# A transformer block on one core: a step order of its own for each engine, from a table of shifts

## What is computed

```python
x = x + layernorm(attention(layernorm(x)))      # 16 heads of 16 channels, rotary, causal softmax
x = x + layernorm(ffn(layernorm(x)))
# ffn(h): router (sigmoid, 4 groups of 4 experts, best 2 groups, best 4 experts of 16)
#         y = sum over the 4 picked experts of gate * (silu(h Wg) * (h Wu)) Wd
#         returns h + y + shared(h), shared(h) = (silu(h Ws_g) * (h Ws_u)) Ws_d
```

## Time and profile before

| what | value |
|---|---|
| median of 3 runs | 983.47 us (982.06 to 987.12) |
| span of the profiled execution | 1048.8 us |
| PE busy | 852.6 us, 81% |
| PEld busy | 615.2 us, 59% |
| DVE busy | 652.3 us, 62% |
| ACT busy | 456.3 us, 44% |
| POOL busy | 426.7 us, 41% |
| mean granted TensorE clock | 0.888 |

### The profile page before, as it was taken

The page is one execution under the profiler, slowest core; times in us unless marked ns, Lnnn a source line. Parts: engine busy times, 40 slices in busy tenths (PEclk is TensorE's granted clock), DMA queues, the critical chain, the costliest instruction groups (busy, mean ns, idle before and its releaser), DMA issues.

```text
span 1048.8 us, 20609 instructions
## 1 busy us (share of the span) xinstructions
PE 852.6 (81%) x6580; PEld 615.2 (59%) x6580; DVE 652.3 (62%) x1914; ACT 456.3 (44%) x763; POOL 426.7 (41%) x408
## 2 busy tenths in 40 slices
PE   4569798987987987987987877978977799989955
PEld 3436374664664663664654545757865588867722
DVE  5577658687687687687586674533642233687916
ACT  2115454544544544544543555425433355544410
POOL 3222113135335335335213234374565555664621
PEclk9759898997897897997987998889999999998978
DMA  4685726236336336336395212453545566997783
GB/s 161 147 222 144 216 64 163 75 98 174 98 99 173 99 99 173 98 81 172 98 322 159 85 47 92 144 167 93 166 150 161 161 178 164 383 314 281 247 339 128
DMA packets 89175, 168.72 MB, mean 161 GB/s; under 512 B 14704, under 2 KB 56688, under 8 KB 88816
## 3 DMA queue, kind: packets, MB, share of 16 engines
q1 hardware_dynamic: 75248, 128.85, 42.1%
q0 software_dynamic: 13824, 38.55, 9.9%
HBM read 90.15 MB, written 76.68 MB: 159 GB/s over the span
## 4 chain that ended last, share of the span: by engine, by line
PE 40%; DVE 23%; issue 11%; SPq 8%; DMA 6%; another core or an unknown queue 5%; ACT 4%; POOL 3%; DVEq 0%; ACTq 0%; POOLq 0%
DVE nmax L829 8%; PE ring L1536 6%; PE ring L1314 5%; PE ring L1316 4%; PE ring L1315 4%; PE ring L1392 3%; PE ring L1557 3%; PE ring L1358 2%; SPq L628 2%; PE ring L1383 2%; SPq L629 2%; DMA xg<-sorted_rows 2%; PE ring L1436 2%; PE ring L1522 2%
## 5 line engine op out<-in xcount | busy, mean ns | idle before, releaser
L1244 ACT ACTIVATE prob<-ring 128x1024 f32<-128x1024 f32 (+1 forms) x192 | 167.5, 881 | 215.5 <-PE ring L1383 196.5
L829 DVE TENSOR_REDUCE nmax<-ring 128x2 f32<-128x1024 f32 (+3 forms) x256 | 201.8, 819 | 73.3 <-PE ring L1365 43.6
L736 POOL DMA_INDIRECT expert_rows<-ys,dest x160 | 159.2, 995 | 127.0 <-ACT ys L1198 74.8
L728 POOL DMA_INDIRECT sorted_rows<-xr,idx_all x128 | 130.5, 1019 | 104.8 <-DVE xr L991 71.5
L1536 PE MATMUL ring<-we,xh 128*128 x640 | 160.3, 396 | 0.0
L1536 PEld LDWEIGHTS ring<-we,xh 128*128 128x128 f32 x640 | 121.6, 200 | 14.6
L1054 DVE SCALAR_TENSOR_TENSOR sl<-sl,got,ring 128x128 f32<-128x128 f32 x160 | 48.3, 343 | 109.8 <-ACT sl L1296 62.5
L1358 PE MATMUL ring<-k_st,q_st 48*128 48x512 f32 (+3 forms) x512 | 88.9, 387 | 26.0 <-issue 9.7
L1392 PE MATMUL ring<-prob,v_sb 128*32 128x512 f32 (+3 forms) x1024 | 106.3, 518 | 3.2 <-ACT prob L1244 3.2
L1377 PE MATMUL ring<-maskt_b,halves_b 64*128 64x128 bf16 (+2 forms) x768 | 58.4, 233 | 50.7 <-DVE nmax L829 23.5
L1377 PEld LDWEIGHTS ring<-maskt_b,halves_b 64*128 64x128 bf16 x768 | 22.8, 97 | 125.4 <-issue 56.7
(11 more groups left out here) (203 smaller groups left out, 1650.8 us busy)
## 6 DMA issues: line engine op xcount, KB each, us to landing
xg<-sorted_rows SPq DMA_DIRECT2D x160, 134.0 KB
parts<-part SPq DMA_DIRECT2D x32, 512.0 KB
ykt<-expert_rows SPq DMA_DIRECT2D x14, 1024.0 KB
k_st<-parts SPq DMA_DIRECT2D x64, 128.0 KB
q_st<-parts SPq DMA_DIRECT2D x64, 128.0 KB
we<-w_exp SPq DMA_DIRECT2D x1, 6144.0 KB
sorted_rows<-zeros SPq DMA_DIRECT2D x2, 2144.0 KB, 9.6
sorted_rows<-zeros SPq DMA_DIRECT2D x32, 134.0 KB
```

The lines of the kernel that those rows point to most:

```text
L728: pool.indirect_dma_start(out=xs[group_of(s)], out_offset=bass.IndirectOffsetOnAxis(ap=idx_all[:, s, t, k:k + 1], axis=0), in_=xr[:, s % 2 ...
L736: pool.indirect_dma_start(out=yk, out_offset=bass.IndirectOffsetOnAxis(ap=dest[:, j % 8, b:b + 1], axis=0), in_=ys[:, j % NYS, b, :], in_o ...
L829: dve.tensor_reduce(nmax[:, Q % 2, :, pp, qb], slot[:, :, col:col + (qb + 1) * P], AX.X, ALU.max, negate=True).then_inc(s_max, 1)
L1244: act_e.activation(prob[:, u % 2, 2 * half:2 * half + 2, 0:width], slot[:, :, 0:width], ACT.Exp, scale=SCALE).then_inc(s_exp, 1)
```

## The change

A table `MOVES` gives shifts in the units of the list. A key is (kind and part, engine or None for all, quad of the sequence 0 to 3 or None, sequence or None); the shifts of all keys that match are added. `make_plan` is now called once per engine, so each engine sorts its own list. Which quad or sequence a step belongs to comes from its number; the kinds in `FIXED_KINDS` (expert blocks, final sums, `DUM`, `PAD`, `WE`, `GE`, `GR`) don't move. No instruction is added, taken away or changed in size. The ring's rotation and PE's waits for it follow PE's list, the number that a DVE maximum waits for follows PE's list, and so on: each wait is counted in the order of the engine that raises it.

```diff
-def make_plan():
+MOVES = {
+    (('AT',), 'tensor', None, None): 0.01, (('AT',), 'vector', None, None): 0.1, (('AV', 0), 'tensor', 3, None): 0.5,
+    (('AV', 0), 'tensor', None, None): 0.1, (('AV', 0), None, None, None): 0.03, (('AV', 1), 'tensor', 1, None): 0.6,
...
+    (('GA', 0), 'scalar', None, None): -0.7, (('GA', 0), 'gpsimd', None, 7): -1.8, (('GA', 0), None, None, None): 0.5,
...
+    (('LG',), 'scalar', None, None): 0.2, (('LN',), 'gpsimd', None, None): 1.5, (('LNA',), 'vector', None, 7): -0.9,
+    (('LNA',), 'vector', None, None): -1.3, (('LNA',), 'gpsimd', None, None): -2.2, (('LNA',), None, None, None): 0.2,
+    (('LNB',), 'vector', None, 7): -0.7, (('LNB',), 'vector', None, None): -0.2, (('LNB',), None, None, None): -0.1,
+    (('LNC',), 'sync', None, None): -2.0, (('LNC',), None, None, None): 0.6, (('LNR',), 'scalar', None, None): 2.3,
...
+    (('LX',), 'sync', None, None): -2.7, (('MT',), 'vector', 3, None): -0.2, (('MT',), 'sync', None, None): 0.3,
+    (('MT',), None, 1, None): 0.11, (('MT',), None, None, 0): -0.16, (('MT',), None, None, 7): -0.2,
+    (('MT',), None, None, None): -0.1, (('OP',), None, None, None): -0.2, (('OT',), 'vector', 0, None): 0.2,
+    (('OT',), 'vector', 1, None): 0.3, (('OT',), 'vector', None, None): 0.2, (('OT',), None, 0, None): -1.5,
...
+    (('S', 1, 1), None, None, None): 0.15, (('S', 1, 2), None, 1, None): 0.2,
...
+    (('SC', 3, 3), None, None, None): 2.8, (('SPL', 0), 'gpsimd', None, None): -1.4, (('SPL', 0), None, None, 7): 0.5,
...
+    (('STL',), 'sync', None, 7): 0.9, (('STL',), 'sync', None, None): 1.08, (('STL',), None, 0, None): -0.3,
...
+    (('XT',), 'scalar', None, 1): -0.7, (('XT',), None, None, None): 0.5,
+    (('Z',), 'sync', None, None): 1.3, (('Z',), None, None, None): -0.1,
+}
+QUAD_KINDS = ("S", "ST", "AV", "OT", "MT", "STL")
+FIXED_KINDS = ("BT1", "BGU", "BT2", "BDN", "BLD", "CZ", "CL", "CA", "CS", "CN", "DUM", "WE", "GE", "GR", "PAD")
+ENGINES = ("tensor", "vector", "scalar", "gpsimd", "sync")
+
+def moved(engine, step):
+    if step[0] in FIXED_KINDS:
+        return 0.0
+    key = (step[0],) + step[2:]
+    quad, s = (step[1] % QUADS, step[1] // QUADS) if step[0] in QUAD_KINDS else (None, step[1])
+    places = [(key, e, q, n) for e in (None, engine) for q in {None, quad} for n in (None, s)]
+    return sum(MOVES.get(p, 0.0) for p in places)
+
+def make_plan(engine):
     timed = []
     def add(time, *step):
-        timed.append((time, len(timed), step))
+        timed.append((round(time + moved(engine, step), 6), len(timed), step))
...
-PLAN = make_plan()
+PLAN = {engine: make_plan(engine) for engine in ENGINES}
...
-S_DONE = {st[1:]: i + 1 for i, st in enumerate([st for st in PLAN if st[0] == "S"])}
-MAX_DONE = running("S", S_PARTS)
-ST_DONE = {st[1:]: i + 1 for i, st in enumerate([st for st in PLAN if st[0] == "ST"])}
+S_DONE = {st[1:]: i + 1 for i, st in enumerate([st for st in PLAN["tensor"] if st[0] == "S"])}
+MAX_DONE = running("S", S_PARTS, "vector")
+ST_DONE = {st[1:]: i + 1 for i, st in enumerate([st for st in PLAN["scalar"] if st[0] == "ST"])}
...
-            for st in PLAN:
+            for st in PLAN["sync"]:
```

More of the change, by code:

```diff
@@ L136, in sooner @@
     return {"LN": -24, "LNR": -22.7, "XT": -16.9}.get(kind, time) if s == 1 else time
-def make_plan():
+MOVES = {
[9 rows of a table added]
+    (('LG',), 'scalar', None, None): 0.2, (('LN',), 'gpsimd', None, None): 1.5, (('LNA',), 'vector', None, 7): -0.9,
+    (('LNA',), 'vector', None, None): -1.3, (('LNA',), 'gpsimd', None, None): -2.2, (('LNA',), None, None, None): 0.2,
+    (('LNB',), 'vector', None, 7): -0.7, (('LNB',), 'vector', None, None): -0.2, (('LNB',), None, None, None): -0.1,
+    (('LNC',), 'sync', None, None): -2.0, (('LNC',), None, None, None): 0.6, (('LNR',), 'scalar', None, None): 2.3,
+    (('LNR',), None, None, None): 1.0, (('LNS',), 'gpsimd', None, None): -0.2, (('LNS',), None, None, None): -0.2,
[37 rows of a table added]
+    (('SC', 3, 3), None, None, None): 2.8, (('SPL', 0), 'gpsimd', None, None): -1.4, (('SPL', 0), None, None, 7): 0.5,
+    (('SPL', 1), None, None, 0): 2.0, (('SPL', 1), None, None, None): 0.5, (('SPS', 0), 'sync', None, 1): -1.1,
+    (('SPS', 0), 'sync', None, None): 0.4, (('SPS', 1), 'sync', None, 1): -0.3, (('SPS', 1), 'sync', None, 7): -1.8,
[5 rows of a table added]
+    (('ST', 1, 1), 'scalar', 1, None): 0.5, (('ST', 1, 2), None, None, None): 0.1, (('STL',), 'sync', 0, None): -0.4,
+    (('STL',), 'sync', None, 7): 0.9, (('STL',), 'sync', None, None): 1.08, (('STL',), None, 0, None): -0.3,
+    (('STL',), None, None, 7): -1.12, (('STL',), None, None, None): 0.5, (('V',), None, None, None): 0.2,
[3 rows of a table added]
+}
[10 more added lines that the diff above has]
+def make_plan(engine):
     timed = []
     def add(time, *step):
-        timed.append((time, len(timed), step))
+        timed.append((round(time + moved(engine, step), 6), len(timed), step))
     per_seq = 3 * QUADS
@@ L181, in make_plan, with running @@
     return [step for _, _, step in sorted(timed)]
-PLAN = make_plan()
-def running(kind, parts):
+PLAN = {engine: make_plan(engine) for engine in ENGINES}
+def running(kind, parts, engine):
     n, done = 0, {}
-    for st in PLAN:
+    for st in PLAN[engine]:
         if st[0] == kind:
@@ L207, in chain @@
     slot, before, last, blocks, i = {}, {}, [None] * n, False, 0
-    for st in PLAN:
+    for st in PLAN["tensor"]:
         blocks = blocks or st[0] == "BT1"
@@ L750, in _ @@
             pool.wait_ge(s_init, 8)
-            for st in PLAN:
+            for st in PLAN["gpsimd"]:
                 kind, n = st[0], st[1]
@@ L1110, in _ @@
             routes = {}
-            for st in PLAN:
+            for st in PLAN["vector"]:
                 kind, n = st[0], st[1]
@@ L1198, in copy @@
                 act_e.activation(dst, src, ACT.Copy).then_inc(done, 1)
-            for st in PLAN:
+            for st in PLAN["scalar"]:
                 kind, n = st[0], st[1]
```

## The result

The changed kernel takes 944.6 us (median of 4 runs, 940.8 to 948.5), the kernel before 983.9 beside it. The ratio is 0.9599, with a 95% interval of 0.9562 to 0.9635. The forecast was 966, a gain of 1.8%; the gain is 4.0%. That is inside the range (938 to 985) and 3 us from the second case, 942, which had a chance of 0.22; but the gain, 39.3 us, is over twice the 17.4 that the sum gave.

What follows compares the result with a forecast made beforehand. It took the bound to alternate in a period, DVE about a third, PE the rest. Terms 7.6 (SP) + 12 (PE and DVE) - 1 (new waits) = 18.6 us of profile, scaled by 0.938 to 17.4: 966 us, range 938 to 985.

Steps and rivals of the forecast that it cites:

- the second case: Six steady periods: PE's low clock, tied to its waits, recovers too; 6.3 us a period, 942 us, chance 0.22.
- ACT's moves follow PE's: 0: ACT's list in the new order: its moves follow PE's, so they were counted as 0 us.
- SP's first two waits: Start, PE waiting for maxima rows ahead of quads 0 and 4: net gains 3.5 and 4.1, together 7.6 us.
- the quad-4 wait: PE's 6.05 us ahead of quad 4's first `ST`; 4.1 us gain, nothing if zeros ahead in the DMA ring hold it.
- The ring and `LNA`: Six steady periods: new home rotation, `LNA` filling DVE's idle 1.23 and 0.74 us; 2.0 a period, 12 in all.
- POOL (0): POOL's steps jump one to five scatters; none of the listed PE and DVE waits is for POOL, so 0 us.
- New waits at `S` (1,1): PE, `S` (1,1) inheriting its home from `S` (1,0) waits for DVE's maximum: 1 us over the kernel, bounds 0 and 10.
- the full stretch: About a third of each period where DVE bounds: busy 9.82 of 10 us, PE 6.22 at clock 0.65.
- The expert stage (0): Expert blocks, from 660 us on: their steps don't move, so the stage stays as long as before.
- The slower rival: Periods: `LNA` ahead of maxima and rotary products on DVE holds PE; 1.6 us a period lost, 990 us, chance 0.17.
- The clock case: Periods: `LNA`'s 2.1 us leave DVE's busiest stretch and PE regains 2.2 of clock; 6.3 a period, 942 us, chance 0.22.
- the first case: The forecast itself: 2.0 us a period from DVE's idle time, 966 us, chance 0.45.

## Why the forecast was right in direction and too small

The step that failed is the sum's "ACT's moves follow PE's: 0": ACT's list is worth 15 to 17 us of the 39. Beside it the term of PE and DVE, 12 less 1 (10.3 scaled), was too small: their lists alone gave 17.9 us. Term by term:

**SP's first two waits (7.6 us of the profile, 7.1 scaled).** The mechanism was right, the size somewhat high. Quad 8 begins 3.8 to 5.5 us sooner with SP's list than without it. The new wait at quad 6 was forecast at 2.1 and is 1.88; that at quad 1 at 3.0 and is 5.02. What the step lacked: it needs other lists beside it, by the trace ACT's, for alone it gives nothing. The Trainium skill (DMA: Bandwidth & Descriptors, section on queues, rings and completion order) has descriptors consumed in ring order, and the prediction concluded that the quad-4 wait would then stay. It went, but this does not test the rule: in the changed kernel the zeros are issued at 107.56 and land 9.6 us later, at about 117.2, and `MT` 4's rows are issued from 116.81 to 119.9, so hardly anything of the zeros was still ahead of them. The zeros, and the store ahead of quad 1's stack, do cost time where they are: moving both gave 0.8%.

**The ring and `LNA` (12 us of the profile, 11 scaled).** Right in size where it was measured alone: 9.5 us (1.0%). The step "I don't count these waits but DVE's idle time that they open" agrees with that for the old kernel with these two groups of keys. It failed as the total of the periods: the five took 22.0 us less, 4.4 each and not 2.0, and the last attention stage, with the sixth of the steady periods in it, 9.7 less. Most of that does not need ACT: with the lists of PE and DVE alone the five already take 18.7 us less than before (345.4 against 364.1 between DVE's first maxima of quads 8 and 28). Which of PE's and DVE's other moves (`MT`, `OT`, `S` (0,2), `LNB`, `XT`) give the part beyond the two groups was not taken apart. With the other moves in place DVE's stretch does lose `LNA`'s time, which the prediction had as the condition of its second case.

**ACT (0).** The step that failed most. "ACT's moves follow PE's: 0" was written without pricing one of them; the list is worth 1.6 to 1.7%. What the runs show in its place are two waits of a queue, neither of which explains the whole. At the start, with SP's new list and ACT's old one, an exponential stands behind a split whose input is late (2.59 us on ACT), its `ST` home comes late, and PE waits 2.62 us at an `S`. In the periods, with ACT's old order, `OP`'s copies stand behind the splits, so `LNA` and the rotary products behind it come late and PE waits 1.60 us instead of 0.68. The wait of 1.98 at `S` (0,1) was left out of the sum too; it names ACT, but it went with PE's and DVE's lists. The larger part of what ACT's list gives is open.

**POOL (0), router.** POOL's zero was right. The router's moves were not priced; they are worth a few us at most, by a difference of medians that the intervals don't tell from nothing.

**New waits at `S` (1,1) (1 us).** With the ring's keys alone it was 2.74 us a period in the full stretch, in place of 0.61 and 2.02 ahead of two `ST`. In the changed kernel there is none from quad 8 to quad 27. But there is one of its kind that the prediction did not see:

```profile
492.14 0.79 PE L1440 MATMUL ring<-k_st,q_st 48*128 48x512 f32 x2 [4.71 <-DVE nmax L911]
```

This is `S` (0,0) of quad 28. In the new rotation it takes its home from `S` (1,1) of quad 27 (before, from an `ST`), and that maximum begins only at 490.80: `LNA` and some 4 us of small instructions for the tables of group 0 stand ahead of it in DVE's queue. With it PE's waits ahead of an `S` for a maximum add up to 8.0 us from quad 2 on, where before there were none: not the 1 us of the sum, but within its bound of 10.

**The expert stage (0).** Wrong by 5.8 us. Its steps don't move, but steps of sequence 7 are mixed in: with their own keys taken out the stage is as long as before (185.2 us against 183.7).

**The slower rival.** Its wait appeared where it was put, `ST` (1,2) behind the rotary products, with 0.68 us against the 0.9 forecast, and decides nothing. With ACT's old order it is 1.55 to 1.60.

**The clock case.** It gave 942 and the result is 944.6, and its condition (`LNA` leaves the stretch outright) was met. That the number comes so near is in part luck: its 6.3 us a period are the 2.0 of the first case with 2.1 of `LNA` and 2.2 of the clock, so it has `LNA`'s work in it twice; the period took 4.4 us less, where it had 5.9 scaled; and 5.8 us came from the expert stage, which it had at nothing. Of the 43 us between the two profiles 10.8 are PE's busy time, a quarter. The Trainium skill (TensorE: Matmul & The Clock Gate, Part 1) has activity lift the gate, and the rows agree: the clock of the stretch rose from 0.66 to 0.99 as PE's idle share there fell from 38 to 30%. The case was given too little weight because the full stretch kept its work in my reading; the undoing of `LNA` shows that it did not.

## What to carry to other kernels

When several queues hang together through shared homes, price the moves of every engine, also of one that is busy under half of the time: what counts is which late input its queue puts ahead of a result that somebody waits for. A part can be worth more in the new version than in the old one (`LNA`'s keys 0.5% there, 1.0 to 1.2% here), so undo parts of the new version as well as adding parts to the old one. Don't take a wait's name for its cause: the one that named ACT went with the lists of two other engines. And check a profile's span against the median of the runs before reading sizes from it.

## What the hardware showed unexpectedly

One execution of the unchanged kernel took 1048.8 us under the profiler and another 982.0; in the first, PE, ACT and DVE stopped together once a period (for 2.45, 3.77 and 4.31 us at 332 us). And the same 6580 matmuls kept PE busy for 820.2 us in one kernel and 809.4 in the other, at a mean granted clock of 0.919 and 0.940.
